# An LSTM's gate biases folded into its input weights, and one tanh over all four gates in place of four

## The reference, cut to what matters

```python
h = tokens(x)                                  # [128 images, 65 tokens, 128]
h = h + lstm(layernorm(h), W_ih, W_hh, b_ih, b_hh)
h = h + experts(layernorm(h), ...)             # top 2 of 16

def layernorm(x, eps=1e-5):                    # no scale, no shift: its 128 outputs sum to zero
    return (x - mean(x)) / sqrt(var(x) + eps)

def lstm(x, W_ih, W_hh, b_ih, b_hh):           # 65 steps, one after the other
    xg = einsum('btd,gd->btg', x, W_ih) + b_ih + b_hh
    def step(h, c, xt):
        i, f, g, o = split(xt + h @ W_hh.T, 4)
        c = sigmoid(f) * c + sigmoid(i) * tanh(g)
        h = sigmoid(o) * tanh(c)
```

## Time and profile before

| | |
|---|---|
| Median of three runs | 673.26 us |
| The profiled execution's own time | 674.92 us |
| Its span, from first to last instruction | 673.1 us |
| Busy: PE, DVE, ACT, POOL | 619.0, 562.3, 489.7, 411.9 us |

### The profile page before, as it was taken

How to read it: one execution, slowest core, us unless ns; L and a number is a source line. 1 busy time by engine, 2 the same in 40 slices (tenths; PEclk the granted TensorE clock), 3 DMA queues, 4 the chain that set the end, 5 groups by cost and what they waited for, 6 DMA issues and landing times.

```text
span 673.1 us, 24553 instructions
## 1 busy us (share of the span) xinstructions
PE 619.0 (92%) x7952; PEld 587.0 (87%) x7952; DVE 562.3 (84%) x1797; ACT 489.7 (73%) x1259; POOL 411.9 (61%) x446
## 2 busy tenths in 40 slices
PE   4899999999999999999998967999999999999970
PEld 4899999999999999999998856788888898888860
DVE  3887888888888888988989878997787887889896
ACT  3687877666677666665665457778888888999883
POOL 0233333477677776667656677777777666666571
PEclk9999999999999999999999989999999999999995
DMA  8987887688888888877876113445554445555675
GB/s 308 384 285 272 267 274 251 235 265 273 267 277 273 265 274 255 247 238 260 263 245 205 52 54 100 112 130 169 165 142 115 120 114 158 156 174 160 188 224 201
DMA packets 71895, 141.67 MB, mean 210 GB/s; under 512 B 13078, under 2 KB 55650, under 8 KB 63838
## 3 DMA queue, kind: packets, MB, share of 16 engines
q1 hardware_dynamic: 62128, 121.69, 58.1%
q0 software_dynamic: 9280, 17.21, 7.3%
q10 hardware_dynamic: 366, 1.21, 0.5%
HBM read 116.35 MB, written 25.66 MB: 211 GB/s over the span
## 4 chain that ended last, share of the span: by engine, by line
PE 57%; DVE 8%; issue 6%; DMA 5%; POOL 3%; ACT 1%; SPq 0%; POOLq 0%; ACTq 0%; DVEq 0%
PE pair L1281 22%; PE pair L1436 11%; PE pair L1454 11%; PE pair L1327 4%; DMA patches<-sent 4%; PE pair L1291 3%; PE pair L1410 2%; DVE patches L1099 2%; PE pair L1296 1%; POOL back L1259 1%; PE pair L1382 1%; DMA field<-back 1%; POOL sent L1235 1%; PE pair L1353 1%; PE pair L1316 1%
## 5 line engine op out<-in xcount | busy, mean ns | idle before, releaser
L1259 POOL DMA_INDIRECT back<-patches x160 | 156.7, 979 | 69.0 <-issue 54.7
L1281 PE MATMUL pair<-field,patches 128*128 128x128 f32 (+1 forms) x1408 | 173.7, 280 | 9.2 <-DMA patches<-in_x 9.2
L1235 POOL DMA_INDIRECT sent<-pay,slot_own x130 | 148.9, 1146 | 40.0 <-issue 37.0
L1281 PEld LDWEIGHTS pair<-field,patches 128*128 128x128 f32 (+1 forms) x1408 | 164.4, 194 | 9.5 <-issue 8.0
L680 ACT ACTIVATE pair<-pair,b1s 128x256 f32<-128x256 f32 x320 | 123.1, 448 | 29.0 <-PE pair L1436 28.3
L605 ACT ACTIVATE gate<-pair,lbias 128x128 f32<-128x128 f32 x260 | 74.1, 367 | 81.4 <-PE pair L1296 79.5
L1247 POOL TENSOR_TENSOR rstd<-veps,cst 128x2 f32<-128x2 f32 (+1 forms) x68 | 57.4, 844 | 94.7 <-DVE veps L800 94.2
L1436 PE MATMUL pair<-patches,ex_hi 128*128 128x256 f16 x640 | 109.8, 274 | 6.0 <-DVE patches L1099 3.7
L1454 PE MATMUL pair<-ex_hi,patches 128*128 x1280 | 111.4, 219 | 2.9 <-DVE patches L1099 1.5
L1099 DVE TENSOR_TENSOR patches<-pair,patches 128x1024 f16<-128x1024 f32 x80 | 97.2, 1215 | 1.7 <-ACT patches L689 1.7
L1281 PE MATMUL pair<-field 128*128 128x128 f16 x1536 | 96.1, 219 | 0.0
(11 more groups left out here) (150 smaller groups left out, 1232.2 us busy)
## 6 DMA issues: line engine op xcount, KB each, us to landing
patches<-in_x SPq DMA_DIRECT2D x62, 1152.0 KB
patches<-sent SPq DMA_DIRECT2D x80, 130.0 KB
field<-in_we SPq DMA_DIRECT2D x64, 128.0 KB
field<-back SPq DMA_DIRECT2D x10, 768.0 KB, 5.2
patches<-in_b SPq DMA_DIRECT2D x80, 64.0 KB
field<-in_pos SPq DMA_DIRECT2D x65, 64.0 KB
out_tower<-h SPq DMA_DIRECT2D x10, 384.0 KB
back<-patches POOLq DMA_INDIRECT x160
```

Of the source, the lines that this page charges most:

```text
L1235: pool.indirect_dma_start(sent, bass.IndirectOffsetOnAxis(ap=slot_own[:, g % 4, choice, col:col + 1], axis=0), pay[:, t % NP, :], None, bo ...
L1259: pool.indirect_dma_start(back, bass.IndirectOffsetOnAxis(ap=dsti[j % NO][:, k:k + 1], axis=0), yo[j % NO][:, k, :], None, bounds_check=2 ...
L1281: last = pe.matmul(bank_of, l, w_, start=(c == KS and k == 0), stop=(c == KS - 1 and k == 2))
```

## The change

Layernorm's 128 outputs sum to zero, so the first is minus the sum of the others, and W x = sum over j>0 of (W_j - W_0) x_j. Column 0 of the normalised token is then free: it is set to 1 once, and the first row of the input weights becomes b_ih + b_hh. Row 0 is subtracted from the other rows. The g gate's weights are doubled, so that all gates take the scale 0.5, and one tanh of 128x512 does what four of 128x128 did. The gates stand in another order in the bank, so that the two products of the cell state still lie side by side.

New at the start are: a DMA that copies row 0 of `w_ih` to all 128 partitions; two DMAs that gather the biases into one partition, turned from [128, 4] to [4, 128], in place of two that wrote them as they lie; and on DVE a subtraction of 128x512, an addition of 1x512 and two doublings of 128x128. ACT waits for the last of these, where it waited for the DMAs.

```diff
-        lbias = sb("lbias", [HID, 3, 4])
+        wih_first = late[:, (KS + 8) * HID:(KS + 12) * HID].rearrange("p (a b) -> p a b", a=4)
+        brow = late[0:1, (KS + 12) * HID:(KS + 20) * HID].rearrange("p (k a b) -> p k a b", k=2, a=4)
-        GATE_AT = (1, 0, 4, 2)
-        c2 = gate[:, 3, :]
+        GATE_AT = (1, 2, 3, 0)
+        c2 = gate[:, 4, :]
@@ SP, slot -4
-                    for dst, src in ((wih[:, :, :], w_ih), (whh[:, :, :], w_hh),
-                                     (lbias[:, 0, :], b_ih), (lbias[:, 1, :], b_hh)):
+                    for dst, src in ((wih[:, :, :], w_ih),
+                                     (wih_first, w_ih[0:1, :, :].rearrange("a g h -> (a g h)").partition_broadcast(P)
+                                      .rearrange("p (g h) -> p g h", g=4)),
+                                     (whh[:, :, :], w_hh)):
                         sp.dma_start(dst, src).then_inc(weights_in, 16)
+                    for k, src in enumerate((b_ih, b_hh)):
+                        sp.dma_start(brow[:, k], src.rearrange("h g -> g h").unsqueeze(0),
+                                     allow_slow_non_contiguous=True).then_inc(weights_in, 16)
@@ ACT, recurrent_weights
-                act.wait_ge(weights_in, 16 * N_WEIGHTS)
+                act.wait_ge(setup_dve, 5)
@@ ACT, step
-                    for g in range(4):
-                        last = act.activation(gate[:, GATE_AT[g], :], ps_gate[n % 2][:, g * B:(g + 1) * B], ACT.Tanh,
-                                              bias=lbias[:, 2, g:g + 1],
-                                              scale=(1.0 if g == 2 else 0.5) / G_SCALE)
-                    last.then_inc(gates_done, 1)
+                    act.activation(gate[:, 0:4, :].rearrange("p g b -> p (g b)"), ps_gate[n % 2], ACT.Tanh,
+                                   scale=0.5 / G_SCALE).then_inc(gates_done, 1)
@@ DVE, once, and in slot -2 ahead of constants_in
+            dve.memset(xn[:, :, 0:1], 1.0)
+            def bias_in_weights():
+                dve.wait_ge(weights_in, 16 * N_WEIGHTS)
+                flat = wih.rearrange("p a b -> p (a b)")
+                dve.tensor_tensor(flat, flat, wih_first.rearrange("p a b -> p (a b)"), ALU.subtract).then_inc(setup_dve, 1)
+                dve.wait_ge(setup_dve, 3)
+                dve.tensor_tensor(wih[0:1, :, :], brow[:, 0], brow[:, 1], ALU.add).then_inc(setup_dve, 1)
+                dve.wait_ge(setup_dve, 4)
+                dve.tensor_scalar(wih[:, 2, :], wih[:, 2, :], 2.0, None, ALU.mult)
+                dve.tensor_scalar(whh[:, 2, :], whh[:, 2, :], 2.0, None, ALU.mult).then_inc(setup_dve, 1)
@@ DVE, constants_in
-                dve.wait_ge(weights_in, 16 * N_WEIGHTS)
-                dve.tensor_tensor(lbias[:, 2, :], lbias[:, 0, :], lbias[:, 1, :], ALU.add).then_inc(setup_dve, 1)
-                dve.wait_ge(setup_dve, 3)
-                dve.tensor_tensor(lbias[:, 2, :], lbias[:, 2, :], cst[:, C_BSC:C_POW], ALU.mult).then_inc(setup_dve, 1)
@@ DVE, step
-                    dve.tensor_scalar(xn[:, t0 % 2, :], src0, mv[:, 0, 0:1], rstd[:, 0:1], ALU.subtract,
+                    dve.tensor_scalar(xn[:, t0 % 2, 1:HID], h0[:, t0 % 4, 1:HID], mv[:, 0, 0:1], rstd[:, 0:1], ALU.subtract,
                                       ALU.mult).then_inc(xn_done, 1)
@@ PE: the matmuls of a gate g write column GATE_AT[g] * B of the bank, not g * B; their order stays
```

More of the change, by code:

```diff
@@ L313, in tower @@
         out_done = sem("out_done")
-        N_FIRST, N_WEIGHTS, N_CONST = 2, 4, 3
+        N_FIRST, N_WEIGHTS, N_CONST = 2, 5, 3
         R_MASK, R = 12, 16
@@ L601, in step @@
                     through(act, gates_ps, n)
-                    if n == 0:
-                        act.wait_ge(setup_dve, 4)
-                    for g in range(4):
-                        last = act.activation(gate[:, GATE_AT[g], :], ps_gate[n % 2][:, g * B:(g + 1) * B], ACT.Tanh,
-                                              bias=lbias[:, 2, g:g + 1],
-                                              scale=(1.0 if g == 2 else 0.5) / G_SCALE)
-                    last.then_inc(gates_done, 1)
+                    act.activation(gate[:, 0:4, :].rearrange("p g b -> p (g b)"), ps_gate[n % 2], ACT.Tanh,
+                                   scale=0.5 / G_SCALE).then_inc(gates_done, 1)
                 t = token_at(transposes_y, n)
@@ L803, in step @@
                     through(dve, gates_done, n)
-                    dve.scalar_tensor_tensor(cab[:, :, :], gate[:, 0:2, :], 1.0, gate[:, 3:5, :], ALU.add,
+                    dve.scalar_tensor_tensor(cab[:, :, :], gate[:, 1:3, :], 1.0, gate[:, 3:5, :], ALU.add,
                                              ALU.mult).then_inc(cab_done, 1)
                     through(dve, cab_done, n)
-                    dve.scalar_tensor_tensor(c2, cab[:, 0, :], 0.5, cab[:, 1, :], ALU.mult, ALU.add).then_inc(c_done, 1)
+                    dve.scalar_tensor_tensor(c2, cab[:, 1, :], 0.5, cab[:, 0, :], ALU.mult, ALU.add).then_inc(c_done, 1)
                     routing(n)
@@ L825, in step @@
                     through(dve, tc_done, n)
-                    dve.scalar_tensor_tensor(h2_hi[:, n % 2, :], gate[:, 2, :], 1.0, tc[:, :], ALU.add,
+                    dve.scalar_tensor_tensor(h2_hi[:, n % 2, :], gate[:, 0, :], 1.0, tc[:, :], ALU.add,
                                              ALU.mult).then_inc(h_hi_done, 1)
-                    dve.scalar_tensor_tensor(h2[:, n % 2, :], gate[:, 2, :], 1.0, tc[:, :], ALU.add,
+                    dve.scalar_tensor_tensor(h2[:, n % 2, :], gate[:, 0, :], 1.0, tc[:, :], ALU.add,
                                              ALU.mult).then_inc(h_done, 1)
@@ L845, in step @@
                 if n == -2:
+                    bias_in_weights()
                     constants_in()
@@ L1290, in step @@
                         for w_ in (whh_hi, whh_lo):
-                            pe.matmul(here[:, g * B:(g + 1) * B], w_[:, g, :], h2_hi[:, (n - 1) % 2, :],
+                            pe.matmul(here[:, GATE_AT[g] * B:(GATE_AT[g] + 1) * B], w_[:, g, :], h2_hi[:, (n - 1) % 2, :],
                                       start=False, stop=False, skip_group_check=True)
@@ L1295, in step @@
                     for g in range(4):
-                        last = pe.matmul(here[:, g * B:(g + 1) * B], whh_hi[:, g, :], h2_lo[:, (n - 1) % 2, :],
+                        last = pe.matmul(here[:, GATE_AT[g] * B:(GATE_AT[g] + 1) * B], whh_hi[:, g, :], h2_lo[:, (n - 1) % 2, :],
                                          start=False, stop=True, skip_group_check=True)
@@ L1321, in step @@
                         pe.wait_ge(setup_act, 3)
-                        pe.wait_ge(setup_dve, 6)
+                        pe.wait_ge(setup_dve, 7)
                     if t >= 2:
@@ L1326, in step @@
                         for k, (w_, r) in enumerate(((wih_hi, xT_hi), (wih_hi, xT_lo), (wih_lo, xT_hi))):
-                            pe.matmul(ps_gate[t % 2][:, g * B:(g + 1) * B], w_[:, g, :], r[:, t % 2, :],
+                            pe.matmul(ps_gate[t % 2][:, GATE_AT[g] * B:(GATE_AT[g] + 1) * B], w_[:, g, :], r[:, t % 2, :],
                                       start=(g == 0 and k == 0), stop=False, skip_group_check=True)
```

## The result

The changed kernel takes 679.83 us (median of 4, 678.76 to 680.98), the kernel before 673.35 (median of 4, 672.86 to 674.25). The ratio of the runs is 1.0091, with a 95% interval from 1.0071 to 1.0111 (the two medians alone give 1.0096). The change makes the kernel slower: by 6.5 us between the medians, 6.1 by the ratio, where 6.95 had been worked out, and inside the range.

The account below looks back on a forecast made before the run. Bound by a start of chained arrivals, a long stretch filled by PE, and a short one where DVE's order counts too. Late gate 5.65 + clock 1.5 - steps 0.2 = 6.95 us on 673.1: 680.1 us, range 675.6 to 687.2.

Parts of the forecast that it names:

- The weights' arrival: Start: row copy adds 0.60 us, bias packets on four engines 3.60; weights there at 21.54 us instead of 17.34.
- Token 3's patches: Start: these patches come some 4 us late by the same packets, but hidden, since PE needs them later.
- The chain: Start, behind the weights: four new DVE instructions take 1.94 us, then ACT's conversions and DVE's remainder, to PE's gate.
- The gate: Start: PE's first input gate at 26.64 us instead of 20.99, +5.65 us.
- The clock: Start: PE resumes at 1.2 GHz after 8.2 us of standing still, costing 1.5 us, between 0 and 2.3.
- The steps: LSTM steps: the single tanh saves ACT 35 us but the path only 0.2 us, between 0 and 4.3.
- The sum: Whole kernel: 5.65 + 1.5 - 0.2 = 6.95 us more, 680.2 us on the median.
- Packets: Sign in the profile: 768 more packets under 512 B from the turned biases.
- Rival 1: Start: small packets are cheap, shared by 16 engines; weights at 18.66 us, total 676.0 to 677.5; chance 0.22.
- rival 2: Start: packets are dear, 42 ns on four engines; weights at 28.45 us, total 687.2, or 691.8 on one engine; chance 0.14.
- Rival 3: Start: the stall is absorbed or the weights never were late, so nothing changes, 673.3 us; chance 0.04.
- rival 4: Steps from 350 us on: bound by the recurrence through the tanh, 4.3 us won, total 671.9; chance 0.04.

Follow-up runs that it names:

- e3: The kernel before with only the one tanh and its gate order, without the bias folding and the doubling of one gate's weights: 673.75 us, ratio 1.0012.
- e8: The kernel before with only the preparation at the start reordered for a shorter chain: 674.12 us, ratio 1.0009.
- f2: e8 with 35 unneeded matmuls in PE's idle time before the first input gate: 675.41 us, ratio 1.0020.
- e2: The changed kernel with four tanh of 128x128 again, in the new gate order: 681.38 us, ratio 1.0111.
- e4: The changed kernel with 125 unneeded matmuls keeping PE busy before the first input gates: 677.28 us, ratio 1.0057.
- e5: The changed kernel with both biases gathered a second time into a spare row, which the weights also wait for: 683.63 us, ratio 1.0166.
- e6: The changed kernel with the two bias gathers issued on POOL instead of SP: 680.94 us, ratio 1.0122.
- e7: The changed kernel with biases contiguous in DRAM and the preparation at the start reordered for a shorter chain: 673.63 us, ratio 1.0013.
- g1: e7 unchanged, run again beside g2 on one chip: 674.50 us, ratio 1.0011.
- e1: The changed kernel with the biases laid out as 4 x 128 in DRAM, so each arrives as one row: 676.82 us, ratio 1.0048.
- f1: e7 with 62 unneeded matmuls in PE's idle time before the first input gate: 677.22 us, ratio 1.0065.
- g2: f1 unchanged, run again beside g1 on one chip: 678.06 us, ratio 1.0063.

## Why the prediction was right

- **The weights' arrival.** Said: 21.54 us, 4.20 later than before. Measured: 20.92, 3.58 later, in this pair of traces. Executions differ: where the DMAs are those of the kernel before, the work on the weights starts at 17.34, 16.67, 16.64 and 17.00 us (before, e3, e8, f2), and where they are those of the change at 20.92, 21.14 and 21.04 (after, e2, e4). Between the means are 4.1 us. So the size was right, and that was in part luck, for the mechanism was not. I had the packets spread over four engines of a full queue, costing their engine time, 10 to 25 ns each. They take 8.7 ns, below that span. By my own sum two gathers then are 256 x 8.7 ns = 2.2 us, less 0.24, and the arrival, with 0.60 for the row, 2.6 us late. The rest is what the sum had not: SP itself was held for 8.92 us in the issue of the second gather, the queue ran dry behind it, and one gather's burst followed the other's, with 1.5 us between them in which almost nothing moved. A price too high stood in for a wait that was left out. e5's 2.2 us a gather is what it costs; four engines are not shown. Nor does any run show the 0.60 us of the row.
- **Token 3's patches.** "Some 4 us late" by the packets; they were issued 8.8 us late, by SP (17.00 for 8.24). Hidden, as said: the burst that needs them at 31.25 has no wait. e6 shows the other side: there patches that had no such cover came late.
- **The chain.** Said: 1.94 for DVE's four, 5.10 us to PE's gate. Measured: 20.92 to 22.82, 1.90, and 5.03. The row with one partition and 512 elements took 0.68 us, as the one with 128.
- **The gate.** Said 26.64, measured 25.95, by the first point.
- **The clock.** Said +1.5 of 0 to 2.3, measured +1.33 by the trace and about 1.6 by e4. The upper end was read from two bursts as two clock levels, but the profile grants 1.00 in both (8 to 13 and 14 to 17 us), so for the first the level is not shown by the clock's row. e6 has the same burst at a granted 0.50, in 5.07 us, which bears the 2.3 out.
- **The steps.** Said -0.2, 0 to -4.3. Measured -0.60 by the pair of traces, -0.8 between the means of all 14: the tenths on PE's side were more, still far from -4.3. The tanh was there 0.54 us sooner each time, and what follows wasn't: amid the projection

```profile
208.40 0.60 ACT L608 ACTIVATE gate<-pair 128x512 f32<-128x512 f32 x1 [1.32 <-PE pair L1306]
209.45 0.17 DVE L809 TENSOR_SCALAR veps<-mv 128x2 f32<-128x2 f32 x1
209.53 0.42 DVE L813 SCALAR_TENSOR_TENSOR cab<-gate 128x256 f32<-128x256 f32 x1
```

  the gates end at 209.00 and `cab` starts at 209.53 behind `veps`, as in the earlier trace rows; in the step at 360.94 they end at 361.54 and `cab` starts at 362.85.
- **The sum.** Said +6.95; measured +5.69 at the LSTM's end and +6.48 between the medians. The 0.8 us between these two have no known cause: behind the LSTM two executions of one kernel differ by 1.8 us (270.7 in e7, 272.5 in g1).
- **Packets.** Said 768 more under 512 B, measured 760 (13838 less 13078).

Rival 1 (weights by 18.66) and rival 2 (28.45) are refuted by DVE's start on the weights at 20.92, before 19 or after 25 being their signs; rival 2's 42 ns also by the 8.7. Rival 1's premise, that more than four engines share the packets, is open. Rival 3 is refuted by the 5.69 us that were still there at the LSTM's end, rival 4 by `cab` standing behind DVE's order and by e3.

## What to carry to other kernels

A DMA that turns a tiny array is paid by its elements, 2.2 us for 512 here, and by what stands behind it on the issuing engine; turn the array where it is laid out (here 0.43% of 0.91%, 2.9 us). Folding work into the weights moves it ahead of the first use of them, and at the start nothing covers that; order the preparation by what the first user needs (2.4 us more, by the ratios). Taking 35 us off an engine that isn't waited for was worth 0.8 us, and the place to see that beforehand is what its reader was queued behind. A trace is one execution: e1's and f1's took 2.7 and 2.9 us less than the median of their own runs, as much as the effects in question.

## What was not expected of the hardware

- A DMA of 512 elements of 4 B took the issuing engine 0.80 us, the next one like it 8.92 us while the queue still held larger transfers, and 1.33 us each once those had drained (e5). Nothing was issued from that engine meanwhile.
- TensorE's second burst of the kernel, the same 22 matmuls, took 2.72 us in nine of the profiled executions, where 0.92 to 1.54 us of idling stood ahead of it, and 4.29 to 4.35 in four (e1, e2, e4, g2), where it was 1.72 to 2.31. (e6, with 4.13 us, took 5.07.) The idling is the arrival of the patches, which varies between executions of one kernel: f1 and g2 are the same, with 2.72 and 4.35. So one trace of the first 30 us shows one of several courses, and an edit tuned to one of them, as the count of 62 matmuls, can lose in the other.
- Before the input gates it was otherwise: 1.98 us of idling and the lower clock (e8), 2.53 and 3.74 us and the higher one (before, e1). The length of the gap alone doesn't tell.
